# Deformable convolution, layer 2: convolution tiles split by tap parity, x planes and even taps on ScalarE

## The chip, the core and the metric

The kernel runs on one core of a Trainium2 chip. A core has TensorE for matrix products (PE in the rows: its weight loads stand apart as PEld), VectorE (DVE), ScalarE (ACT), GpSimd (POOL) and SyncE (SP), which here only starts transfers. The engines run their own instruction lists and meet at semaphores. The metric is the device time of one execution of the whole program in microseconds.

## What is computed

Four layers run on a batch of 4 images of 64 channels by 48 x 48 pixels. The change touches the second one only. In that layer two deformable 3x3 convolutions (index v below) read the same image, each with its own offsets:

```python
def deform_conv(x, offset, w, b):
    off = offset.reshape(B, K2, 2, H, W)
    dy, dx = (off[:, :, 0], off[:, :, 1])
    ...
    py = base_y.astype(x.dtype) + dy
    px = base_x.astype(x.dtype) + dx
    sampled = bilinear_gather(x, py, px)
    out = jnp.einsum('bckhw,ock->bohw', sampled, w.reshape(O, C, K2))
    return out + b[None, :, None, None]
```

Each of the 9 taps of each output pixel is a bilinear sample of the image; then a plain product over 64 channels and 9 taps follows, and a bias for each output channel.

## The kernel before

The touched function is `windows1`. It works in 24 chunks (`NQ`, 4 images times 6) of 8 rows by 48 pixels, 384 pixels (`CH`) each. A bilinear sample is written as a product with a small matrix of weights: each tile of 4 x 6 pixels takes its samples from a window of 10 x 12 pixels, so the contraction runs over 120 window places (`KW`), and a weight is the product of a hat function in y and one in x. For one chunk the stages are these.

- **Placement** (`place`, line 1455 on TensorE): two products of 384 columns for each half write the distances of the samples from the window places. ScalarE takes the magnitude (`magnitude`, L1539, 768 columns), VectorE turns it into hats in place (`hats_of`, L1578).
- **Nine steps** t = 0 to 8 (`STEPS`), each for two of the 18 samples (9 taps, two convolutions). `spread` (L1476) is four products of 32 rows by 120 columns of weights and 384 moving columns; they write two y planes to `p_y[t % 2]` and two x planes to `p_x`. Before the weights can be formed, the x planes are copied to `xs`: ScalarE copies plane 0 (`keep_x`, L1546), VectorE plane 1 (L1583). Then VectorE multiplies the y planes in PSUM by the x planes in SBUF (L1588, 768 columns) and writes the sampling weights `bmat`. There is one `p_x` (banks 4 and 5 of PSUM), so the next `spread` waits until both planes are out.
- **Eight sampling products** (`sample`, L1494), four matmuls of 216 columns each, use the weights of the chunk before; ScalarE moves their result to `smp` (`keep`, L1553). In the list of TensorE they alternate with the steps: `spread(n+1, t)`, `sample(n, t)`.
- **The convolution** (`conv`, L1510): for each tap four matmuls on the 64 x 64 quadrants of the array, convolution v on rows 64v, pixel half h on columns 64h, 192 moving columns each. They accumulate over the nine taps in PSUM banks 2 and 3 (`pc[v]`), which are also `p_y[1]`; three taps run before the second placement of chunk n+2, six behind it. VectorE adds the bias and writes the result in four pieces (`biased`, L1597).

An fp32 matmul stands in the records as two passes, with a weight load for each: a `spread` is 8 records, and the 36 matmuls of one `conv` are 72. All orders are written out by hand in the five engine lists; no scheduler moves anything. ScalarE's list in a chunk is `keep_x(n+1, t)`, `keep(n, t)` for t = 0 to 8, then the two magnitudes of chunk n+2. VectorE's is nine times copy and product, two hats, `biased(n)`. Chunk 0 has its nine steps alone in front, and chunk 23 its sampling alone at the end.

Of the kernel before, what the change touches and what calls it, by code (L numbers as in the profile page):

```python
# [6 lines left out]
ALU = mybir.AluOpType  # L7
# [15 lines left out]
TAPS = 9  # L23
# [1384 lines left out]
def windows1(nc, k, o3, bmat, win, sc, smp, hats, xs):  # L1408
# [7 lines left out]
         ("loaded0", "loaded1", "places", "absed", "hats", "spread", "x0_out", "x1_out", "weights", "sampled", "kept", "conv", "sc")}  # L1416
# [10 lines left out]
    pc = [ps[:, 512 * (2 + v):512 * (2 + v) + CH // 2] for v in range(2)]  # L1427
    S4 = smp.rearrange("p (s y x) -> p s y x", s=TAPS, y=ROWS)
    hat = hats.rearrange("p (q n) -> p q n", q=4)

    with nc.Block() as block:
# [14 lines left out]
        def _(pe):  # L1446
            def place(m, half):
                if half == 0:
                    if m >= 2:
                        pe.wait_ge(S["kept"], (m - 1) * PAIRS)  # L1450
                elif m:
                    pe.wait_ge(S["x0_out"], m * STEPS)
                    pe.wait_ge(S["x1_out"], m * STEPS)
# [5 lines left out]
            def spread(m, t):  # L1459
# [3 lines left out]
                else:  # L1463
                    pe.wait_ge(S["x0_out"], g)
                    pe.wait_ge(S["x1_out"], g)
# [14 lines left out]
            def sample(n, i):  # L1480
                if i == 0:
                    pe.wait_ge(S["weights"], (n + 1) * STEPS)
                    pe.wait_ge(S[f"loaded{n % 2}"], 64 * (n // 2 + 1))
                    if n + 1 < NQ:
                        pe.wait_ge(S["absed"], 2 * (n + 2))
# [13 lines left out]
            def conv(n, taps):  # L1499
# [5 lines left out]
                for t in taps:  # L1505
                    for v in range(2):
                        own = slice(64 * v, 64 * v + 64)
                        for h in range(2):
                            at = CH * t + CH // 2 * h
                            mm = pe.matmul(pc[v][64 * h:64 * h + 64, :], k["dws"][own, t, :], smp[own, at:at + CH // 2],  # L1510
                                           start=(t == 0), stop=(t == TAPS - 1), skip_group_check=True)
# [9 lines left out]
            for n in range(NQ):  # L1521
# [5 lines left out]
                if n + 2 < NQ:  # L1527
                    place(n + 2, 0)
                    conv(n, range(0, 3))
                    place(n + 2, 1)  # L1530
                    conv(n, range(3, TAPS))
# [4 lines left out]
        def _(act):  # L1536
# [4 lines left out]
            def keep_x(m, t):  # L1541
# [4 lines left out]
                act.activation(xs[t % 2][:, 0:CH], p_x[:, 0, :], ACT.Copy).then_inc(S["x0_out"], 1)  # L1546

            def keep(n, i):
                band, pair = divmod(i, NTX // 2)
                act.wait_ge(S["sampled"], n * PAIRS + i + 1)  # L1550
                if i == 0 and n:
# [3 lines left out]
                    .then_inc(S["kept"], 1)  # L1555

# [6 lines left out]
            for n in range(NQ):  # L1563
# [5 lines left out]
                if n + 2 < NQ:  # L1569
                    magnitude(n + 2, 0)  # L1570
                    magnitude(n + 2, 1)

        @block.vector
        def _(v_):
            def hats_of(m, half):
                v_.wait_ge(S["absed"], 2 * m + half + 1)
                own = hat[:, 2 * half:2 * half + 2, :]
                v_.tensor_scalar(own, own, 1.0, 1.0, ALU.min, ALU.subtract).then_inc(S["hats"], 1)  # L1578

            def weight(m, t):  # L1580
                g = m * STEPS + t
                v_.wait_ge(S["spread"], g + 1)
                v_.tensor_copy(xs[t % 2][:, CH:2 * CH], p_x[:, 1, :]).then_inc(S["x1_out"], 1)  # L1583
                v_.wait_ge(S["x1_out"], g + 1)
                v_.wait_ge(S["x0_out"], g + 1)
# [1030 lines left out]
```

## Time and profile before

| what | us |
|---|---|
| median of 3 runs | 1517.17 |
| lowest, highest | 1516.56, 1517.31 |
| the profiled execution | 1518.79 |
| its span in the trace | 1517.0 |
| TensorE, VectorE, ScalarE, GpSimd busy in the span | 1226.1, 1058.5, 637.0, 418.1 |
| `windows1` in the span, first placement to last bias | about 399 to 889.4 |

The page gives each engine's busy time, then the span in 40 slices, then groups of instructions. A row of the groups names line, engine, operation, what is written and read, partitions by elements, the count, busy time and mean duration, and behind the bar the idle time ahead of it with its releaser. A row of the timeline gives start, length, engine and count, and in brackets the idle time ahead. The 24 chunks repeat each other closely, so that one chunk can be read for all.

### The profile page before, as it was taken

To read this page: it belongs to the slowest core of one execution; us is meant where nothing else is said; L and a number is where in the kernel's file an instruction comes from. 1 tells how busy PE (TensorE), PEld (TensorE's weight loads), DVE (VectorE), ACT (ScalarE), POOL (GpSimd) and SP (SyncE) were. 2 spreads that over 40 slices of the span, in tenths; PEclk is the share of its full clock that TensorE was granted. 3 is DMA by queue.
4 is the path that set the end of the run, shared out by engine and by line. 5 is a ranking of instruction groups with operands and counts; after the bars stand their busy time and mean duration, and the time that the engine had idled before them with its cause. 6 is when DMAs were issued, how large, how long until landed. Compare 5 with 4: busy or idle time off the path is not lost. (4 is left out here: it accounts for less than half of the span.)

```text
span 1517.0 us, 32058 instructions
## 1 busy us (share of the span) xinstructions
PE 1226.1 (81%) x13604; PEld 605.8 (40%) x13604; DVE 1058.5 (70%) x1310; ACT 637.0 (42%) x1003; POOL 418.1 (28%) x272
## 2 busy tenths in 40 slices
PE   3860089959499999999999958879999999999558
PEld 1430077734134444444444434423333333334233
DVE  2679935568678888888888856864666767676623
ACT  1534035345345555555555524514444444445410
POOL 2001011222100000000000001118888888888400
PEclk9985599979589999999999978779999999999779
DMA  4100000002100000000000000400000000000132
GB/s 81 17 1 0 0 3 3 2 27 58 40 14 28 27 28 27 28 27 28 26 18 25 28 2 0 125 1 1 1 1 2 1 2 2 2 1 2 50 37 64
DMA packets 29071, 31.50 MB, mean 21 GB/s; under 512 B 19340, under 2 KB 21837, under 8 KB 28157
## 3 DMA queue, kind: packets, MB, share of 16 engines
q1 hardware_dynamic: 28925, 29.41, 7.8%
q8 instruction: 109, 1.79, 0.5%
q14 instruction: 37, 0.30, 0.1%
HBM read 21.07 MB, written 5.35 MB: 17 GB/s over the span
## 5 line engine op out<-in xcount | busy, mean ns | idle before, releaser
L2072 POOL TENSOR_TENSOR arena_sb<-arena_sb 128x768 f32<-128x768 f32 x168 | 323.0, 1923 | 121.6 <-ACT arena_sb L2033 101.1
L2087 DVE TENSOR_REDUCE arena_sb<-ps 128x4 f32<-128x1536 f32 x108 | 188.6, 1758 | 129.4 <-PE ps L1929 128.1
L2033 ACT ACTIVATE arena_sb<-ps 128x768 f32<-128x768 f32 x216 | 174.8, 810 | 243.1 <-PE ps L1962 241.0
L1476 PE MATMUL ps<-xp_sb,arena_sb 32*120 32x384 f32 x1728 | 207.0, 549 | 25.0 <-DVE arena_sb L1583 21.9
L1588 DVE TENSOR_TENSOR arena_sb<-ps,arena_sb 120x768 f32<-120x768 f32 x216 | 206.8, 957 | 8.2 <-DVE arena_sb L1583 0.8
L1962 PE MATMUL ps<-arena_sb 33*64 33x384 f32 x1728 | 187.5, 502 | 11.3 <-ACT arena_sb L2033 5.4
L1494 PE MATMUL ps<-arena_sb 120*64 120x216 f32 x1536 | 182.3, 359 | 0.0
L1974 PE MATMUL ps<-arena_sb 64*64 64x384 f32 x1728 | 168.0, 488 | 3.4 <-ACT arena_sb L2040 3.4
L1546 ACT ACTIVATE arena_sb<-ps 120x384 f32<-120x384 f32 x216 | 105.9, 490 | 148.7 <-PE ps L1476 148.7
L1583 DVE COPY arena_sb<-ps 120x384 f32<-120x384 f32 x216 | 120.4, 558 | 43.6 <-PE ps L1476 40.7
L1765 POOL MEMSET arena_sb<- 128x64 f32 x1 | 0.2, 151 | 544.8 <-POOLq L210 544.8
L1494 PEld LDWEIGHTS ps<-arena_sb 120*64 120x64 f32 x1536 | 93.2, 136 | 119.8 <-ACT xp_sb L1553 77.4
L1553 ACT ACTIVATE xp_sb<-ps 128x432 f32<-128x432 f32 x192 | 101.8, 530 | 74.7 <-PE ps L1494 74.7
L1929 PE MATMUL ps<-arena_sb 32*128 32x384 f32 x864 | 110.1, 584 | 15.6 <-DVE arena_sb L2087 9.6
L1476 PEld LDWEIGHTS ps<-xp_sb,arena_sb 32*120 32x120 f32 x1728 | 67.7, 182 | 101.3 <-ACT arena_sb L1546 65.7
L1962 PEld LDWEIGHTS ps<-arena_sb 33*64 33x64 f32 x1728 | 58.1, 134 | 110.1 <-ACT arena_sb L2033 86.0
L1974 PEld LDWEIGHTS ps<-arena_sb 64*64 64x64 f32 x1728 | 67.5, 134 | 78.8 <-issue 72.9
L610 PE MATMUL ps<-ident_sb,arena_sb 128*32 128x128 f32 x576 | 19.3, 289 | 77.9 <-PEq L472 77.9
L1510 PE MATMUL ps<-xp_sb,arena_sb 64*64 64x192 f32 x1728 | 80.8, 328 | 0.7 <-ACT xp_sb L1553 0.6
L1929 PEld LDWEIGHTS ps<-arena_sb 32*128 32x128 f32 x864 | 37.2, 199 | 87.3 <-issue 44.6
L1510 PEld LDWEIGHTS ps<-xp_sb,arena_sb 64*64 64x64 f32 x1728 | 61.8, 133 | 18.7 <-issue 14.0
L1597 DVE TENSOR_SCALAR arena_sb<-ps,dbs_sb 64x192 f32<-64x192 f32 x96 | 39.9, 416 | 27.4 <-PE ps L1510 26.4
(228 smaller groups left out, 1478.0 us busy)
## 6 DMA issues: line engine op xcount, KB each, us to landing
arena_sb<-pixel_major SPq DMA_DIRECT2D x96, 120.0 KB, 2.3
pixel_major<-arena_sb SPq DMA_DIRECT2D x24, 108.0 KB
x_sb<-in_x SPq DMA_DIRECT2D x4, 576.0 KB, 9.1
arena_sb<-arena_sb SPq DMA_DIRECT2D x8, 288.0 KB, 6.0
xn_sb<-in_W SPq DMA_DIRECT2D x1, 2304.0 KB, 8.1
arena_sb<-in_W SPq DMA_DIRECT2D x1, 2304.0 KB, 8.2
out_x<-x_sb SPq DMA_DIRECT2D x24, 96.0 KB, 2.2
arena_sb<-arena_sb SPq DMA_DIRECT2D x16, 36.0 KB, 3.7
```

Source lines behind the costliest of these rows:

```text
L1476: mm = pe.matmul(out, k["spr"][32 * row:32 * row + 32, q, :], hat[32 * row:32 * row + 32, slot, :], start=True, stop=True)
L1494: mm = pe.matmul(out[64 * v:64 * v + 64, :, :, IW * t:IW * t + IW], win[n % 2][0:KW, band, tile, :], weights[:, TAPS * v:TAPS * v + TAPS, ...
L1510: mm = pe.matmul(pc[v][64 * h:64 * h + 64, :], k["dws"][own, t, :], smp[own, at:at + CH // 2], start=(t == 0), stop=(t == TAPS - 1), skip_ ...
L1546: act.activation(xs[t % 2][:, 0:CH], p_x[:, 0, :], ACT.Copy).then_inc(S["x0_out"], 1)
L1583: v_.tensor_copy(xs[t % 2][:, CH:2 * CH], p_x[:, 1, :]).then_inc(S["x1_out"], 1)
L1588: v_.tensor_tensor(bmat[m % 2][:, 2 * CH * t:2 * CH * t + 2 * CH].rearrange("p (e n) -> p e n", e=2), p_y[t % 2], xs[t % 2].rearrange("p ( ...
L1929: mm = pe.matmul(p_m(m)[:, u, :], q4[own, CH * ib + PT * a:CH * ib + PT * a + PT], k4[own, CH * jc:CH * jc + CH], start=True, stop=True)
L1962: mm = pe.matmul(p_scores(g)[64 * i:64 * i + 64, h, :], kp[own, key:key + 64], qp[own, PIX * b2 + CH * ib:PIX * b2 + CH * ib + CH], start= ...
L1974: mm = pe.matmul(p_o[64 * h:64 * h + 64, i, :], at[64 * i:64 * i + 64, b2 * TPI + j, 64 * h:64 * h + 64], pt[g % SLOTS][64 * i:64 * i + 64 ...
L2033: act.activation(pt[g % SLOTS].rearrange("p (h n) -> p h n", h=2), p_scores(g), ACT.Exp)\
L2072: pool.tensor_tensor(acc, first, pt[g % SLOTS], ALU.add).then_inc(S["pool_added"], 1)
L2087: v.tensor_reduce(part.rearrange("p (a u j) -> p a u j", a=3, u=NB)[:, a, :, jc], p_m(m), AX.X, ALU.max)\
```

## The change

- `spread`, `sample` and the placements stay as they are. In `keep_x` ScalarE copies both x planes in one instruction of 768 columns for steps 0 to 7, counted in `x_out` (2 for the two planes). In step 8 the copy is split as before: ScalarE takes plane 0, VectorE plane 1 (`x_half`). VectorE's copies of steps 0 to 7 are gone.
- `conv` has two matmuls for each tap instead of four, one for each convolution, on all 384 columns. Even taps (0, 2, 4, 6, 8) go to the array's columns 0 to 63 and so to PSUM partitions 0 to 63, odd taps (1, 3, 5, 7) to columns and partitions 64 to 127. 18 matmuls in place of 36. Four taps run before the second placement instead of three.
- The two partial sums are now added: `even_taps` on ScalarE copies the even sum with the bias to `sc` (two instructions of 64 x 384), then `biased` on VectorE adds the odd sum (two of 64 x 384, one operand in PSUM and one in SBUF). `biased` waits for `even` in place of `conv`.
- `sample` waits for `hats` where it waited for `absed`; the `spread` just ahead of it waits for the same value already.

TensorE's list around one chunk's turn, before:

```order
456 L1476 MATMUL ps<-xp_sb,arena_sb 120x384 x4
457 L1494 MATMUL ps<-arena_sb 64x36x6 x4
458 L1476 MATMUL ps<-xp_sb,arena_sb 120x384 x4
459 L1455 MATMUL ps<-arena_sb 128x384 x2
460 L1510 MATMUL ps<-xp_sb,arena_sb 64x192 x12
461 L1455 MATMUL ps<-arena_sb 128x384 x2
462 L1510 MATMUL ps<-xp_sb,arena_sb 64x192 x24
463 L1476 MATMUL ps<-xp_sb,arena_sb 120x384 x4
```

The same place of TensorE's list now (L1483 is `spread`, L1501 `sample`, L1463 `place`, L1516 `conv`):

```order
456 L1483 MATMUL ps<-xp_sb,arena_sb 120x384 x4
457 L1501 MATMUL ps<-arena_sb 64x36x6 x4
458 L1483 MATMUL ps<-xp_sb,arena_sb 120x384 x4
459 L1463 MATMUL ps<-arena_sb 128x384 x2
460 L1516 MATMUL ps<-xp_sb,arena_sb 64x384 x8
461 L1463 MATMUL ps<-arena_sb 128x384 x2
462 L1516 MATMUL ps<-xp_sb,arena_sb 64x384 x10
463 L1483 MATMUL ps<-xp_sb,arena_sb 120x384 x4
```

Nothing changes places; the two pieces of the convolution hold 8 and 10 matmuls of 384 columns where they held 12 and 24 of 192.

ScalarE's list at the same turn, before:

```order
277 L1553 ACTIVATE xp_sb<-ps 128x9x4x12
278 L1546 ACTIVATE arena_sb<-ps 120x384
279 L1539 ACTIVATE xp_sb<-ps 128x768 x2
280 L1546 ACTIVATE arena_sb<-ps 120x384
281 L1553 ACTIVATE xp_sb<-ps 128x9x4x12
```

ScalarE's list now (L1553 is the copy of both planes, L1555 that of step 8, L1569 the even taps, L1562 `keep`, L1545 the magnitude):

```order
282 L1562 ACTIVATE xp_sb<-ps 128x9x4x12
283 L1555 ACTIVATE arena_sb<-ps 120x384
284 L1545 ACTIVATE xp_sb<-ps 128x768 x2
285 L1569 ACTIVATE arena_sb<-ps,dbs_sb 64x384 x2
286 L1553 ACTIVATE arena_sb<-ps 120x768
287 L1562 ACTIVATE xp_sb<-ps 128x9x4x12
```

Two instructions with the bias stand ahead of the first copy of the next chunk, and that copy has 768 columns.

VectorE's list at the turn, before, and after it the same place now (L1606 is the product, L1601 the copy of step 8, L1595 the hats, L1614 the adding):

```order
442 L1583 COPY arena_sb<-ps 120x384
443 L1588 TENSOR_TENSOR arena_sb<-ps,arena_sb 120x768
444 L1578 TENSOR_SCALAR xp_sb<-xp_sb 128x768 x2
445 L1597 TENSOR_SCALAR arena_sb<-ps,dbs_sb 64x192 x4
446 L1583 COPY arena_sb<-ps 120x384
447 L1588 TENSOR_TENSOR arena_sb<-ps,arena_sb 120x768
```

```order
381 L1606 TENSOR_TENSOR arena_sb<-ps,arena_sb 120x768 x8
382 L1601 COPY arena_sb<-ps 120x384
383 L1606 TENSOR_TENSOR arena_sb<-ps,arena_sb 120x768
384 L1595 TENSOR_SCALAR xp_sb<-xp_sb 128x768 x2
385 L1614 TENSOR_TENSOR arena_sb<-ps,arena_sb 64x384 x2
386 L1606 TENSOR_TENSOR arena_sb<-ps,arena_sb 120x768 x8
```

Eight products now follow each other without a copy between them, and four additions of a bias became two additions of planes.

The diff:

```diff
--- before.py
+++ after.py
@@ -1413,7 +1413,7 @@
 
     ps = k["psum"]
     S = {n: signal(k, "win_" + n) for n in
-         ("loaded0", "loaded1", "places", "absed", "hats", "spread", "x0_out", "x1_out", "weights", "sampled", "kept", "conv", "sc")}
+         ("loaded0", "loaded1", "places", "absed", "hats", "spread", "x_out", "x_half", "weights", "sampled", "kept", "conv", "even", "sc")}
     NQ = NB * CPI
     NTX = WW // IW
     PAIRS = 2 * (NTX // 2)
@@ -1424,9 +1424,13 @@
     p_x = ps[0:KW, 2048:3072].rearrange("p (e n) -> p e n", e=2)[:, :, 0:CH]
     p_place = [ps[:, at:at + 1024].rearrange("p (e n) -> p e n", e=2)[:, :, 0:CH] for at in (3072, 2048)]
     pq = [ps[:, 512 * (6 + i):512 * (6 + i) + TAPS * IH * 2 * IW] for i in range(2)]
-    pc = [ps[:, 512 * (2 + v):512 * (2 + v) + CH // 2] for v in range(2)]
+    pc = [ps[:, 512 * (2 + v):512 * (2 + v) + CH] for v in range(2)]
     S4 = smp.rearrange("p (s y x) -> p s y x", s=TAPS, y=ROWS)
     hat = hats.rearrange("p (q n) -> p q n", q=4)
+
+    def x_count(steps):
+
+        return 2 * steps - steps // STEPS
 
     with nc.Block() as block:
         @block.sync
@@ -1444,13 +1448,17 @@
 
         @block.tensor
         def _(pe):
+            def x_free(count):
+                pe.wait_ge(S["x_out"], x_count(count))
+                if count >= STEPS:
+                    pe.wait_ge(S["x_half"], count // STEPS)
+
             def place(m, half):
                 if half == 0:
                     if m >= 2:
                         pe.wait_ge(S["kept"], (m - 1) * PAIRS)
                 elif m:
-                    pe.wait_ge(S["x0_out"], m * STEPS)
-                    pe.wait_ge(S["x1_out"], m * STEPS)
+                    x_free(m * STEPS)
                 for e in range(2):
                     mm = pe.matmul(p_place[half][:, e, :], k["selp"][:, 2 * half + e, :], o3[:, CH * m:CH * m + CH],
                                    start=True, stop=True)
@@ -1461,8 +1469,7 @@
                 if t == 0:
                     pe.wait_ge(S["hats"], 2 * (m + 1))
                 else:
-                    pe.wait_ge(S["x0_out"], g)
-                    pe.wait_ge(S["x1_out"], g)
+                    x_free(g)
                 if t < 2 and m:
                     pe.wait_ge(S["weights"], m * STEPS)
                 elif t >= 2:
@@ -1482,7 +1489,7 @@
                     pe.wait_ge(S["weights"], (n + 1) * STEPS)
                     pe.wait_ge(S[f"loaded{n % 2}"], 64 * (n // 2 + 1))
                     if n + 1 < NQ:
-                        pe.wait_ge(S["absed"], 2 * (n + 2))
+                        pe.wait_ge(S["hats"], 2 * (n + 2))
                 if n * PAIRS + i >= 2:
                     pe.wait_ge(S["kept"], n * PAIRS + i - 1)
                 band, pair = divmod(i, NTX // 2)
@@ -1503,12 +1510,11 @@
                         pe.wait_ge(S["sc"], n)
                     pe.wait_ge(S["weights"], (n + 1) * STEPS + (STEPS - 1 if n + 1 < NQ else 0))
                 for t in taps:
+                    h = t % 2
                     for v in range(2):
                         own = slice(64 * v, 64 * v + 64)
-                        for h in range(2):
-                            at = CH * t + CH // 2 * h
-                            mm = pe.matmul(pc[v][64 * h:64 * h + 64, :], k["dws"][own, t, :], smp[own, at:at + CH // 2],
-                                           start=(t == 0), stop=(t == TAPS - 1), skip_group_check=True)
+                        mm = pe.matmul(pc[v][64 * h:64 * h + 64, :], k["dws"][own, t, :], smp[own, CH * t:CH * t + CH],
+                                       start=(t < 2), stop=(t >= TAPS - 2), skip_group_check=True)
                 if taps[-1] == TAPS - 1:
                     mm.then_inc(S["conv"], 1)
 
@@ -1526,9 +1532,9 @@
                         sample(n, t)
                 if n + 2 < NQ:
                     place(n + 2, 0)
-                    conv(n, range(0, 3))
+                    conv(n, range(0, 4))
                     place(n + 2, 1)
-                    conv(n, range(3, TAPS))
+                    conv(n, range(4, TAPS))
                 else:
                     conv(n, range(TAPS))
 
@@ -1543,7 +1549,10 @@
                 act.wait_ge(S["spread"], g + 1)
                 if g >= 2:
                     act.wait_ge(S["weights"], g - 1)
-                act.activation(xs[t % 2][:, 0:CH], p_x[:, 0, :], ACT.Copy).then_inc(S["x0_out"], 1)
+                if t < STEPS - 1:
+                    act.activation(xs[t % 2].rearrange("p (e n) -> p e n", e=2), p_x, ACT.Copy).then_inc(S["x_out"], 2)
+                else:
+                    act.activation(xs[t % 2][:, 0:CH], p_x[:, 0, :], ACT.Copy).then_inc(S["x_out"], 1)
 
             def keep(n, i):
                 band, pair = divmod(i, NTX // 2)
@@ -1553,6 +1562,13 @@
                 act.activation(S4[:, :, IH * band:IH * band + IH, 2 * IW * pair:2 * IW * pair + 2 * IW],
                                pq[i % 2].rearrange("p (s y x) -> p s y x", s=TAPS, y=IH), ACT.Copy)\
                     .then_inc(S["kept"], 1)
+
+            def even_taps(n):
+                act.wait_ge(S["conv"], n + 1)
+                for v in range(2):
+                    last = act.activation(sc.rearrange("p h n -> p (h n)")[64 * v:64 * v + 64, CH * n:CH * n + CH],
+                                          pc[v][0:64, :], ACT.Identity, bias=k["dbs"][0:64, v + 1:v + 2])
+                last.then_inc(S["even"], 1)
 
             magnitude(0, 0)
             magnitude(0, 1)
@@ -1569,20 +1585,22 @@
                 if n + 2 < NQ:
                     magnitude(n + 2, 0)
                     magnitude(n + 2, 1)
+                even_taps(n)
 
         @block.vector
         def _(v_):
             def hats_of(m, half):
+                own = hat[:, 2 * half:2 * half + 2, :]
                 v_.wait_ge(S["absed"], 2 * m + half + 1)
-                own = hat[:, 2 * half:2 * half + 2, :]
                 v_.tensor_scalar(own, own, 1.0, 1.0, ALU.min, ALU.subtract).then_inc(S["hats"], 1)
 
             def weight(m, t):
                 g = m * STEPS + t
-                v_.wait_ge(S["spread"], g + 1)
-                v_.tensor_copy(xs[t % 2][:, CH:2 * CH], p_x[:, 1, :]).then_inc(S["x1_out"], 1)
-                v_.wait_ge(S["x1_out"], g + 1)
-                v_.wait_ge(S["x0_out"], g + 1)
+                if t == STEPS - 1:
+                    v_.wait_ge(S["spread"], g + 1)
+                    v_.tensor_copy(xs[t % 2][:, CH:2 * CH], p_x[:, 1, :]).then_inc(S["x_half"], 1)
+                    v_.wait_ge(S["x_half"], m + 1)
+                v_.wait_ge(S["x_out"], x_count(g + 1))
                 if t == 0 and m >= 2:
                     v_.wait_ge(S["sampled"], (m - 1) * PAIRS)
                 v_.tensor_tensor(bmat[m % 2][:, 2 * CH * t:2 * CH * t + 2 * CH].rearrange("p (e n) -> p e n", e=2),
@@ -1590,13 +1608,10 @@
                     .then_inc(S["weights"], 1)
 
             def biased(n):
-                v_.wait_ge(S["conv"], n + 1)
+                v_.wait_ge(S["even"], n + 1)
                 for v in range(2):
-                    for h in range(2):
-                        at = CH * n + CH // 2 * h
-                        last = v_.tensor_scalar(sc.rearrange("p h n -> p (h n)")[64 * v:64 * v + 64, at:at + CH // 2],
-                                                pc[v][64 * h:64 * h + 64, :], k["dbs"][64 * h:64 * h + 64, v + 1:v + 2], None,
-                                                ALU.add)
+                    own = k["sc"].rearrange("p h n -> p (h n)")[64 * v:64 * v + 64, CH * n:CH * n + CH]
+                    last = v_.tensor_tensor(own, pc[v][64:128, :], own, ALU.add)
                 last.then_inc(S["sc"], 1)
 
             hats_of(0, 0)
@@ -1609,9 +1624,9 @@
                 if n + 1 < NQ:
                     for t in range(STEPS):
                         weight(n + 1, t)
-                if n + 2 < NQ:
-                    hats_of(n + 2, 0)
-                    hats_of(n + 2, 1)
+                    if n + 2 < NQ:
+                        hats_of(n + 2, 0)
+                        hats_of(n + 2, 1)
                 biased(n)
```

## Rows read from the trace of the kernel before

**Rows 1.** Page, the span in 40 slices: busy tenths, and TensorE's granted clock

```profile
PE   3860089959499999999999958879999999999558
PEclk9985599979589999999999978779999999999779
```

**Rows 2.** Stretches: us, busy and count per engine, clock, DMA share, GB/s

```profile
core 0: us, PE busy (x) PEld busy (x) DVE busy (x) ACT busy (x) POOL busy (x), PEclk, DMA share, GB/s
240.00:300.00 60.00, 54.67 (x1202) 45.31 (x1190) 33.70 (x61) 29.10 (x48) 8.23 (x16) 1.00 0.01 2
485.00:868.00 383.00, 368.33 (x4136) 182.75 (x4128) 318.64 (x470) 198.05 (x370) 0.00 (x0) 1.00 0.09 26
```

**Rows 3.** Timeline of one inner step, from 552.6 (start, length, engine, line)

```profile
552.61 0.92 PE L1476 MATMUL ps<-xp_sb,arena_sb 32*120 32x384 f32 x8
553.46 0.95 PE L1494 MATMUL ps<-arena_sb 120*64 120x216 f32 x8
553.60 0.49 ACT L1546 ACTIVATE arena_sb<-ps 120x384 f32<-120x384 f32 x1 [0.34 <-PE ps L1476]
553.60 0.56 DVE L1583 COPY arena_sb<-ps 120x384 f32<-120x384 f32 x1 [0.18 <-PE ps L1476]
554.34 0.30 PEld L1476 LDWEIGHTS ps<-xp_sb,arena_sb 32*120 32x120 f32 x8 [0.32 <-ACT arena_sb L1546]
```

**Rows 4.** Timeline of a chunk's turn, 541 to 549

```profile
541.21 1.21 PE L1510 MATMUL ps<-xp_sb,arena_sb 64*64 64x192 f32 x24
...
542.77 2.18 PE L1510 MATMUL ps<-xp_sb,arena_sb 64*64 64x192 f32 x48
542.88 0.81 ACT L1539 ACTIVATE xp_sb<-ps 128x768 f32<-128x768 f32 x1 [0.76 <-PE ps L1455]
543.72 0.56 DVE L1578 TENSOR_SCALAR xp_sb<-xp_sb 128x768 f32<-128x768 f32 x1 [0.79 <-ACT xp_sb L1539]
544.88 0.30 PEld L1476 LDWEIGHTS ps<-xp_sb,arena_sb 32*120 32x120 f32 x8 [0.28 <-issue]
...
545.02 1.71 DVE L1597 TENSOR_SCALAR arena_sb<-ps,dbs_sb 64x192 f32<-64x192 f32 x4 [0.74 <-PE ps L1510]
...
546.76 0.56 DVE L1583 COPY arena_sb<-ps 120x384 f32<-120x384 f32 x1
...
547.39 0.33 PEld L1476 LDWEIGHTS ps<-xp_sb,arena_sb 32*120 32x120 f32 x8 [1.09 <-issue]
...
548.39 0.49 ACT L1546 ACTIVATE arena_sb<-ps 120x384 f32<-120x384 f32 x1 [1.13 <-PE ps L1476]
```

**Rows 5.** Timeline of two steps of chunk 0, no sampling between them

```profile
404.30 0.52 PEld L1476 LDWEIGHTS ps<-xp_sb,arena_sb 32*120 32x120 f32 x8 [1.90 <-ACT arena_sb L1546]
...
406.03 0.56 DVE L1583 COPY arena_sb<-ps 120x384 f32<-120x384 f32 x1 [0.85 <-PE ps L1476]
...
406.66 0.52 PEld L1476 LDWEIGHTS ps<-xp_sb,arena_sb 32*120 32x120 f32 x8 [1.85 <-ACT arena_sb L1546]
```

**Rows 6.** Groups of the whole span: busy and mean ns, then idle before

```profile
L1539 ACT ACTIVATE xp_sb<-ps 128x768 f32<-128x768 f32 x48 | 38.8, 810 | 23.5 <-PE ps L1455 23.5
```

**Rows 7.** Timeline: two activations with a bias, 384 columns

```profile
336.52 1.05 ACT L1230 ACTIVATE arena_sb<-ps,offb_sb 128x384 f32<-128x384 f32 x2 [11.10 <-PE ps L1185]
```

**Rows 8.** One line, the fourth layer's addition from PSUM: min/median/max ns

```profile
L2280 DVE TENSOR_TENSOR x_sb<-x_sb,ps x24: 545/552/558, 1483.0 to 1513.8; 64x384 f32<-64x384 f32 x24
```

**Rows 9.** Timeline of the third layer: quadrants of 64 x 64 with 384 columns

```profile
1201.36 1.47 PE L1974 MATMUL ps<-arena_sb 64*64 64x384 f32 x16
...
1205.10 1.15 PE L1974 MATMUL ps<-arena_sb 64*64 64x384 f32 x12
```

**Rows 10.** Timeline of the last two chunks' ends

```profile
874.36 3.15 PE L1510 MATMUL ps<-xp_sb,arena_sb 64*64 64x192 f32 x72
...
887.72 1.71 DVE L1597 TENSOR_SCALAR arena_sb<-ps,dbs_sb 64x192 f32<-64x192 f32 x4 [8.44 <-PE ps L1510]
```

## The prediction, made before the changed kernel had run

> **What bounds the kernel now.** I read the slices of the page first. From slice 12 to 23 TensorE is 9 tenths busy or more and its clock is granted in full [rows 1]. The table of stretches says it for the inner chunks alone: 368.33 of 383 us for TensorE (96%), 318.64 for VectorE (83%), 198.05 for ScalarE (52%), clock 1.00 [rows 2]. Shares do not say what a longer instruction on ScalarE costs, so the timeline of one step comes next. The period is 552.61 to 554.34, 1.73 us. `spread` runs until 553.53, `sample` starts at 553.46 and runs until 554.41, and the next `spread` loads its weights at 554.34 [rows 3]. TensorE has no hole. But both copies start at 553.60, 0.99 after the `spread` began, and VectorE's ends at 554.16. Since one `p_x` serves all steps, the next `spread` could start at the earliest 0.07 later, at 554.23. The slack is only 0.11 us. The 0.07 is how long TensorE takes to go on after a copy: 546.76 + 0.56 = 547.32 to 547.39 [rows 4], and 406.03 + 0.56 = 406.59 to 406.66 [rows 5].
>
> A chunk lasts 19.61 us: 2.51 from its first `spread` to the second (544.88 to 547.39 [rows 4]), seven steps of 1.73, and the rest with step 8, placements and convolution. The 2.51 has a hole on TensorE, since VectorE first does its four biases, 1.71 us, and only then the copy [rows 4].
>
> **1. Both planes on ScalarE.** VectorE loses 0.56 us a step, but it was not the last to end a step; TensorE's own work was. ScalarE's copy grows from 0.49 [rows 3] to 768 columns, which take 0.81 from PSUM to SBUF in the same stage [rows 6]. The two planes went out beside each other in 0.56; now they go out one behind the other in 0.81. The path is: weight load to copy 0.99 (with idle time ahead of it 1.00: 547.39 to 548.39 [rows 4]), copy 0.81, on to TensorE 0.07. That is 1.88 instead of 1.73, so +0.15. ScalarE isn't itself full: 0.81 + 0.53 of 1.88; its `keep` follows the end of `sample`, some 1.85 after the `spread`'s start, when the copy has just ended. VectorE's product of 0.96 runs beside it. Seven such intervals a chunk (steps 1 to 8; the first is item 4) in 22 chunks, and six in the chunk in which the clock rises, are 160 x 0.15 = +24.0. Bounds: if TensorE goes on 0.03 after ScalarE, as VectorE does (542.88 + 0.81 = 543.69 to 543.72 [rows 4]), the step is 1.84 and the term +17.6; with 0.10 for the handing over it is +28.8. I take 0.07 since it was read for this very wait.
>
> The Trainium skill, page "TensorEngine Tiling (Array Packing)", section "PSUM Bottleneck", speaks against this part: after tiling, emptying PSUM can become the limit, and both ScalarE and VectorE should be used for it. The rows above agree, 0.56 side by side against 0.81 on one engine.
>
> **2. The same in chunk 0.** There no sampling lies between the steps, and the wait decides already: load to copy 1.73 (404.30 to 406.03), copy 0.56, on 0.07, together 2.36, at half clock [rows 5]. With 0.81 it is 2.61: 8 x 0.25 = +2.0. Nothing hides it.
>
> **3. The convolution.** The records say whether it is held by columns or by instructions. 24 records (three taps) span 1.21 us and 48 span 2.18 [rows 4], 72 span 3.15 [rows 10]: 0.97 for 24, so four quadrants together need 0.162 for a pass of 192 columns, and a tap 0.323. The third layer has just the new shape, 64 x 64 with 384 columns: 16 records in 1.47, 12 in 1.15, so 0.32 for four together [rows 9]. Twice the columns take twice the time; fewer matmuls save nothing. Two taps now fill the four quadrants for 2 x 0.32 = 0.65 us, and nine taps make five rounds, the last with two quadrants idle: 5 x 0.65 = 3.25 against 9 x 0.323 = 2.91, some +0.33 a chunk. In 24 chunks +7.8. It lies on TensorE, the engine without a hole, so all of it counts. Bounds: 0 (should tap 8 find room somewhere) and +12, a round at 0.68.
>
> The Trainium skill has a rule for the other side: the same page, section "Instruction Overhead", gives each matmul about 60 cycles of overhead. As an estimate from that page, 18 matmuls fewer would give back 18 x 25 ns = 0.45 us a chunk, 10.8 in all, and turn this term into about -3. The rows don't show such a cost.
>
> **4. The start of a chunk.** From the first `spread` on: the conv's end reaches the next engine at +0.14 (545.02 [rows 4]); two activations with a bias take 1.05 [rows 7]; on to VectorE 0.03 [rows 4]; two additions of 0.552 from PSUM [rows 8]; on to TensorE 0.07. The second `spread` waits for `sc`, because `p_y[1]` lies on the convolution's banks, so it starts at 0.14 + 1.05 + 0.03 + 1.10 + 0.07 = 2.39. ScalarE's first copy is ready before, at 0.14 + 1.05 + 0.81 = 2.00. Against 2.51 this is -0.12; I take -0.10, 22 times: -2.2. With the two activations at 0.49 each without extra cost the chain is 2.32 (-4.2 in all), with 0.65 each 2.64 (+2.9). VectorE does the first product after the additions, until about 3.3; it is wanted before the third `spread` at 4.3.
>
> **5. Nothing or little.** The fourth tap ahead of the second placement moves that placement, the second magnitude and the second hats by 0.33; the hats end at 544.28 and are wanted at 544.88 [rows 4], and this moves by 0.33 too. `hats` for `absed`: the `spread` in front waits for it anyway. At the end of the last chunk 1.71 [rows 10] becomes 1.05 + 0.03 + 1.10, +0.5; in the chunk before, the even taps hold ScalarE when the first `keep` is due, +0.2. The transfers (DMA share 0.09 [rows 2]) wait for `sampled` alone. No table load is added on ScalarE: the list of instructions has none.
>
> **Sum.** 24.0 + 2.0 + 7.8 - 2.2 + 0.7 = +32.3. The profiled execution took 1518.8 with a span of 1517.0, 1.6 above the median. 1518.8 + 32.3 = 1551.1; against the median, 1517.2 + 32.3 = **1549.5**.
>
> **The rivals.**
> - The step isn't lengthened: TensorE prepares the next `spread` under the copy so that 0.81 fits. For it: 0.15 is little. Against: chunk 0 shows load, copy and wait in series without overlap. Then items 1 and 2 vanish: 1549.5 - 26 = 1523.5.
> - Faster than before: the convolution is held by its matmuls rather than its columns, and halving them halves it. It gives 24 x 1.46 = -35.1 in place of +7.8: 1506.6. For it: each record carries its own weight load. Against: rows 9. It decides from the point where a convolution saves (24.0 + 2.0 - 2.2 + 0.7)/24 = 1.02 us; around that point lies "no change".
> - The parity split doesn't do what it says: the tiles of one tap pair with each other but not with those of the next, since these come later in the list. Then nine taps cost 9 x 0.65 = 5.85, +2.94 x 24 = 70.6 in place of 7.8: 1612. Against: passes of successive `values` matmuls overlap four by four in rows 9.
> - The holes cost clock. A step gets a hole of 0.15 in 1.88, 8%. A stretch with TensorE 91% busy kept clock 1.00 [rows 2], which speaks against it. If 3 of the 24 chunks ran at 1.2 GHz, each up to 19 us longer since TensorE is busy nearly throughout, the time would be up to 1549.5 + 57 = 1606.5.
>
> **How the numbers follow.** Forecast 0.80, step hidden 0.06, convolution halved 0.05, saving near the break-even point 0.03, parity without overlap 0.03, clock 0.03. The bounds of the terms put together (steps -6.4 to +4.8, convolution -7.8 to +4, start of a chunk -2 to +5, and about 3 for where the clock changes fall in other stages) give, not all at one end, 1538 to 1560. This holds the forecast's case nearly whole, and what lies outside is under 2 in 10. A measurement of this kernel tells about 0.2% (3 us) from no change. Faster by more 0.05, within 0.03, slower 0.92.
>
> **What would show it.** Steps: `spread` every 1.88 instead of 1.73, TensorE's idle time ahead of it released by ScalarE's copy, some 0.15 each. Chunk 0: 2.61. Convolution: 20 records in the larger piece, 0.32 for every four, whole 3.25. First interval of a chunk 2.4. VectorE's busy time in the stage down by more than 100 us while the time rises. The prediction is wrong if the step stays at 1.73 or the convolution gets shorter than 2.9.

## The result and the profile after

The changed kernel takes 1556.96 us in the median (1555.26 to 1559.24, 4 runs) against 1517.24 of the kernel before (1516.56 to 1518.8, 4 runs). The ratio is 1.0261 with a 95% interval of 1.0243 to 1.0279: slower by 2.6%, 39.7 us. The span of the profiled execution went from 1517.0 to 1555.6, +38.6.

From the page of the changed kernel, TensorE's and VectorE's slices, then the groups of line, operation, shapes and count, busy and mean ns, and idle time ahead with its releaser:

```profile
PE   3850199868499999999999977689999999999558
DVE  3769845659445555555555546684666666677723
...
L1606 DVE TENSOR_TENSOR arena_sb<-ps,arena_sb 120x768 f32<-120x768 f32 x216 | 206.8, 957 | 174.9 <-ACT arena_sb L1553 172.2
...
L1553 ACT ACTIVATE arena_sb<-ps 120x768 f32<-120x768 f32 x192 | 155.5, 810 | 120.1 <-PE ps L1483 95.1
...
L1483 PEld LDWEIGHTS ps<-xp_sb,arena_sb 32*120 32x120 f32 x1728 | 67.4, 182 | 139.1 <-ACT arena_sb L1553 121.5
```

The same slices of VectorE in the kernel before:

```profile
DVE  2679935568678888888888856864666767676623
```

The stage is recognisable by VectorE, which falls from 8 tenths to 4 and 5. Its products wait 172.2 us for ScalarE's copies. That by itself costs nothing, since VectorE isn't the engine that holds the step; what counts is the last row, where the weight loads of the next `spread` wait for the same copies. The 192 copies of two planes take 0.810 each, as the magnitudes do in [rows 6]. The stretch that [rows 2] shows of before, now:

```profile
485.00:868.00 383.00, 356.22 (x3192) 147.15 (x3192) 205.20 (x254) 249.82 (x381) 0.00 (x0) 1.00 0.08 24
```

In 383 us VectorE works 205.20 instead of 318.64, ScalarE 249.82 instead of 198.05, and TensorE 356.22 instead of 368.33 at the same full clock. TensorE, which had no hole inside a step, has holes there now. One step, to be laid beside [rows 3]:

```profile
561.78 0.92 PE L1483 MATMUL ps<-xp_sb,arena_sb 32*120 32x384 f32 x8
562.63 0.95 PE L1501 MATMUL ps<-arena_sb 120*64 120x216 f32 x8
562.82 0.81 ACT L1553 ACTIVATE arena_sb<-ps 120x768 f32<-120x768 f32 x1 [0.56 <-PE ps L1483]
563.63 0.53 ACT L1562 ACTIVATE xp_sb<-ps 128x432 f32<-128x432 f32 x1
563.66 0.96 DVE L1606 TENSOR_TENSOR arena_sb<-ps,arena_sb 120x768 f32<-120x768 f32 x1 [0.94 <-ACT arena_sb L1553]
563.68 0.30 PEld L1483 LDWEIGHTS ps<-xp_sb,arena_sb 32*120 32x120 f32 x8 [0.49 <-ACT arena_sb L1553]
```

The period is 561.78 to 563.68, 1.90 us (before 1.73). ScalarE's copy ends at 563.63, and 0.05 later TensorE loads the next weights; `sample` had ended at 563.58, and ahead of the weight load the loader's idle time has grown from 0.32 to 0.49. The chunk's turn, to be laid beside [rows 4]:

```profile
551.43 1.52 PE L1516 MATMUL ps<-xp_sb,arena_sb 64*64 64x384 f32 x16
...
553.32 2.15 PE L1516 MATMUL ps<-xp_sb,arena_sb 64*64 64x384 f32 x20
...
555.40 0.30 PEld L1483 LDWEIGHTS ps<-xp_sb,arena_sb 32*120 32x120 f32 x8 [0.60 <-DVE xp_sb L1595]
...
555.52 1.16 ACT L1569 ACTIVATE arena_sb<-ps,dbs_sb 64x384 f32<-64x384 f32 x2 [1.28 <-PE ps L1516]
...
556.71 1.13 DVE L1614 TENSOR_TENSOR arena_sb<-ps,arena_sb 64x384 f32<-64x384 f32 x2 [1.89 <-ACT arena_sb L1569]
...
557.96 0.33 PEld L1483 LDWEIGHTS ps<-xp_sb,arena_sb 32*120 32x120 f32 x8 [1.15 <-ACT arena_sb L1553]
```

The convolution's first piece, with four taps instead of three, spans 1.52 where it spanned 1.21; the second, with five instead of six, 2.15 where it spanned 2.18. From the first `spread` to the second it is 555.40 to 557.96, 2.56 (before 2.51). A whole chunk went from 19.62 to 21.13.

### The profile page after: what moved, and what is told of

Same layout as the page of the kernel before. It is cut to its first block and busy times, and to the rows that moved or that the text cites. A ratio compares the mean times of both kernels' runs of the same rounds, so it can differ in the third digit from the quotient of the medians.

```text
span 1555.6 us, 29969 instructions
## 1 busy us (share of the span) xinstructions
PE 1249.5 (80%) x12740; PEld 576.6 (37%) x12740; DVE 938.8 (60%) x1070; ACT 723.6 (47%) x1051; POOL 418.1 (27%) x272
## 5 line engine op out<-in xcount | busy, mean ns | idle before, releaser
L1606 DVE TENSOR_TENSOR arena_sb<-ps,arena_sb 120x768 f32<-120x768 f32 x216 | 206.8, 957 | 174.9 <-ACT arena_sb L1553 172.2
L1483 PE MATMUL ps<-xp_sb,arena_sb 32*120 32x384 f32 x1728 | 206.9, 549 | 44.2 <-DVE arena_sb L1614 17.4
L1553 ACT ACTIVATE arena_sb<-ps 120x768 f32<-120x768 f32 x192 | 155.5, 810 | 120.1 <-PE ps L1483 95.1
L1501 PE MATMUL ps<-arena_sb 120*64 120x216 f32 x1536 | 182.3, 359 | 0.2 <-ACT xp_sb L1562 0.2
L1501 PEld LDWEIGHTS ps<-arena_sb 120*64 120x64 f32 x1536 | 93.2, 136 | 120.2 <-ACT xp_sb L1562 77.6
L1944 PE MATMUL ps<-arena_sb 32*128 32x384 f32 x864 | 115.4, 610 | 11.3 <-DVE arena_sb L2102 5.3
L1483 PEld LDWEIGHTS ps<-xp_sb,arena_sb 32*120 32x120 f32 x1728 | 67.4, 182 | 139.1 <-ACT arena_sb L1553 121.5
L1562 ACT ACTIVATE xp_sb<-ps 128x432 f32<-128x432 f32 x192 | 101.7, 530 | 3.1 <-PE ps L1501 2.6
L1516 PE MATMUL ps<-xp_sb,arena_sb 64*64 64x384 f32 x864 | 87.7, 493 | 0.8 <-ACT xp_sb L1562 0.6
L1614 DVE TENSOR_TENSOR arena_sb<-ps,arena_sb 64x384 f32<-64x384 f32 x48 | 26.9, 560 | 54.3 <-ACT arena_sb L1569 53.9
L1545 ACT ACTIVATE xp_sb<-ps 128x768 f32<-128x768 f32 x48 | 38.9, 812 | 30.3 <-PE ps L1463 30.3
L1185 PE MATMUL ps<-xp_sb,offw_sb 64*64 64x384 f32 x432 | 39.9, 516 | 9.4 <-PEq L210 9.4
```

Source lines behind the costliest of these rows:

```text
L1483: mm = pe.matmul(out, k["spr"][32 * row:32 * row + 32, q, :], hat[32 * row:32 * row + 32, slot, :], start=True, stop=True)
L1501: mm = pe.matmul(out[64 * v:64 * v + 64, :, :, IW * t:IW * t + IW], win[n % 2][0:KW, band, tile, :], weights[:, TAPS * v:TAPS * v + TAPS, ...
L1553: act.activation(xs[t % 2].rearrange("p (e n) -> p e n", e=2), p_x, ACT.Copy).then_inc(S["x_out"], 2)
L1562: act.activation(S4[:, :, IH * band:IH * band + IH, 2 * IW * pair:2 * IW * pair + 2 * IW], pq[i % 2].rearrange("p (s y x) -> p s y x", s=T ...
L1606: v_.tensor_tensor(bmat[m % 2][:, 2 * CH * t:2 * CH * t + 2 * CH].rearrange("p (e n) -> p e n", e=2), p_y[t % 2], xs[t % 2].rearrange("p ( ...
L1944: mm = pe.matmul(p_m(m)[:, u, :], q4[own, CH * ib + PT * a:CH * ib + PT * a + PT], k4[own, CH * jc:CH * jc + CH], start=True, stop=True)
```

## The experiments

Each is compared with the kernel before on its own chip. The starts of the x copies in each trace give the step and the whole chunk, in us, alike in nearly all chunks:

| kernel | ratio to before | inner step | chunk |
|---|---|---|---|
| before | 1 | 1.73 | 19.62 |
| the changed kernel | 1.0261 | 1.90 | 21.13 |
| changed, copies count by one | 1.0184 | 1.85 | 20.79 |
| changed, tap 8 in halves | 1.0200 | 1.90 | 20.85 |
| convolution alone | 1.0141 | 1.73 | 20.51 |
| copies alone | 1.0120 | 1.90 | 20.25 |
| before, copies count by two | 1.0007 | 1.73 | 19.62 |
| before, biases split | 0.9882 | 1.73 | 18.81 |
| biases split, placements together | 0.9887 | 1.73 | 18.81 |

**The wait that doesn't fit.** In the changed kernel the copy of two planes starts 1.04 us after its `spread` (561.78 to 562.82), where both old copies and the copy of step 8 start after 0.99. In the records of the changed kernel a wait instruction for the `spread` stands by itself ahead of this copy; the other copies carry that wait themselves. The difference in the source is the increment by 2. On ScalarE a wait instruction (for `weights`) stands ahead of the copy in every kernel, so there is no instruction more: with the increment by 2 it holds the wait for the `spread` too, and the copy itself waits for nothing.

```diff
-        return 2 * steps - steps // STEPS
+        return steps
...
-  act.activation(xs[t % 2]..., p_x, ACT.Copy).then_inc(S["x_out"], 2)
+  act.activation(xs[t % 2]..., p_x, ACT.Copy).then_inc(S["x_out"], 1)
```

> The changed kernel, except that the copy of both x planes raises x_out by 1 instead of 2, and the waits count steps. Theory: the increment by 2 costs the instruction its own wait; a separate wait instruction stands ahead of it, and the copy starts 1.04 us after the spread instead of 0.99. Then the step falls from 1.90 to 1.85, and 168 steps x 0.05 = 8.4 give 1548.6. Rival: the 0.05 belongs to the reading of two planes (768 columns in two banks); then nothing moves, 1557.

Measured: 1548.37 against 1520.05 of the kernel before on that chip, ratio 1.0184 (1.0167 to 1.0201). One step of this kernel:

```profile
558.75 0.92 PE L1483 MATMUL ps<-xp_sb,arena_sb 32*120 32x384 f32 x8
559.74 0.81 ACT L1553 ACTIVATE arena_sb<-ps 120x768 f32<-120x768 f32 x1 [0.45 <-PE ps L1483]
560.60 0.30 PEld L1483 LDWEIGHTS ps<-xp_sb,arena_sb 32*120 32x120 f32 x8 [0.44 <-ACT arena_sb L1553]
```

0.99, 0.81 and 0.05: the step is 1.85. The stretch from the first x copy to the last fell from 507.30 to 498.83, 8.5 us less; the theory had 8.4. Of the 8.5, 0.3 is a single long step that only the changed kernel's trace has (see the last section); 8.2 come from one number in the source, 0.05 in each of the 168 steps. The 0.05 belongs to the separate wait, and reading two banks costs nothing extra. By the two ratios it is 0.8% of 1517, 11.7 us; the intervals of the ratios leave room for 8.5.

**The same number where there is slack.** The kernel before, with both split copies counting by two.

```diff
-  act.activation(xs[t % 2][:, 0:CH], p_x[:, 0, :], ACT.Copy).then_inc(S["x0_out"], 1)
+  act.activation(xs[t % 2][:, 0:CH], p_x[:, 0, :], ACT.Copy).then_inc(S["x0_out"], 2)
-  v_.tensor_copy(xs[t % 2][:, CH:2 * CH], p_x[:, 1, :]).then_inc(S["x1_out"], 1)
+  v_.tensor_copy(xs[t % 2][:, CH:2 * CH], p_x[:, 1, :]).then_inc(S["x1_out"], 2)
```

> The kernel before, with both split copies raising their semaphores by 2 and all their waits doubled; the work is the same. Theory: each copy now starts 1.04 us after its spread instead of 0.99 on ScalarE, and later on VectorE too if it behaves alike. In a step VectorE's copy then ends at 1.60 and TensorE could go on at 1.67, still under the 1.73 of its own work: steps stay 1.73. Only where the wait decides does the time grow: chunk 0 by 8 x 0.05, and at the first step of a chunk nothing where the wait is long fulfilled. 1517.6, no change that can be measured. Rival: there is no slack in the step and 168 x 0.05 = 8.4 come on top, 1525.6.

Measured: ratio 1.0007 (0.9996 to 1.0018), no change. The step in its timeline:

```profile
552.12 0.92 PE L1476 MATMUL ps<-xp_sb,arena_sb 32*120 32x384 f32 x8
552.97 0.95 PE L1494 MATMUL ps<-arena_sb 120*64 120x216 f32 x8
553.16 0.49 ACT L1546 ACTIVATE arena_sb<-ps 120x384 f32<-120x384 f32 x1 [0.39 <-PE ps L1476]
553.18 0.56 DVE L1583 COPY arena_sb<-ps 120x384 f32<-120x384 f32 x1 [0.18 <-PE ps L1476]
553.77 0.96 DVE L1588 TENSOR_TENSOR arena_sb<-ps,arena_sb 120x768 f32<-120x768 f32 x1
553.85 0.30 PEld L1476 LDWEIGHTS ps<-xp_sb,arena_sb 32*120 32x120 f32 x8 [0.32 <-ACT arena_sb L1546]
```

The copies start at 1.04 and 1.06 now, VectorE's ends at 553.74, and the step is still 1.73. The two delays are real and cost an ordinary step nothing, because 0.11 of slack was there. In chunk 0, where the wait decides, the step rose from 2.37 to 2.43. The stretch from the first x copy to the last still grew from 470.8 to 473.0, too little to show in the ratio: 0.6 in chunk 0, 0.5 in chunk 1, and the rest in five single steps that took 1.81 to 2.06.

**The convolution alone.** The kernel before with the new convolution, even taps and additions; the x planes are copied one by each engine as before.

```diff
-  for h in range(2):
-      at = CH * t + CH // 2 * h
-      mm = pe.matmul(pc[v][64 * h:64 * h + 64, :], k["dws"][own, t, :], smp[own, at:at + CH // 2], start=(t == 0), ...)
+  h = t % 2
+  mm = pe.matmul(pc[v][64 * h:64 * h + 64, :], k["dws"][own, t, :], smp[own, CH * t:CH * t + CH], start=(t < 2), ...)
```

> The kernel before with the new convolution, even taps on ScalarE and odd taps added by VectorE, and the x planes copied one by each engine as before. Theory (columns set the convolution): +0.29 us a chunk on TensorE, 7.0 in all; and VectorE's first copy of a chunk now stands behind even taps and additions, 0.14 + 1.16 + 0.03 + 1.13 + 0.56 + 0.07 = 3.09 us in place of 2.51, 22 x 0.58 = 12.8; with 0.7 at the end 1517.2 + 20.5 = 1537.7. Rival (matmuls set the convolution, 60 cycles each): 10.8 less, 1527. Rival (the convolution is halved): 1496.

Measured: 1541.14, ratio 1.0141 (1.0124 to 1.0158); on the 1517.24 of before that is 1538.6, as the column theory has it. Its turn of a chunk:

```profile
546.97 0.30 PEld L1476 LDWEIGHTS ps<-xp_sb,arena_sb 32*120 32x120 f32 x8 [0.60 <-DVE xp_sb L1585]
...
547.09 1.16 ACT L1559 ACTIVATE arena_sb<-ps,dbs_sb 64x384 f32<-64x384 f32 x2 [1.28 <-PE ps L1509]
...
548.28 1.13 DVE L1603 TENSOR_TENSOR arena_sb<-ps,arena_sb 64x384 f32<-64x384 f32 x2 [1.89 <-ACT arena_sb L1559]
...
549.45 0.56 DVE L1590 COPY arena_sb<-ps 120x384 f32<-120x384 f32 x1
...
550.08 0.33 PEld L1476 LDWEIGHTS ps<-xp_sb,arena_sb 32*120 32x120 f32 x8 [1.70 <-issue]
```

The diff shows the convolution alone; `even_taps` and the additions are those of the changed kernel. Even taps, additions and copy stand one behind the other, and the second `spread` comes 3.11 after the first. Both rivals with cheaper matmuls fall: 1527 would have been a ratio of 1.0065, and 1496 one below 1.

**Where the convolution's loss sits.** The changed kernel, with tap 8 computed in two halves of 192 columns, one on each column half of the array.

```diff
+  if t < TAPS - 1:
...
+      continue
+  for h in range(2):
+      at = CH // 2 * h
+      mm = pe.matmul(pc[v][64 * h:64 * h + 64, at:at + CH // 2], k["dws"][own, t, :], smp[own, CH * t + at:CH * t + at + CH // 2], start=False, stop=True, ...)
```

> The changed kernel, with tap 8 alone computed in two halves of 192 columns on both column halves of the array (four matmuls), so that no quadrant is idle in the last round; the sum over both planes stays the same. Theory (two idle quadrants in the fifth round are the whole loss of the convolution): its larger piece is 0.32 us shorter, 24 x 0.32 = 7.7 less than the changed kernel: 1549.3, ratio 1.0210. Rival (the loss comes from 384-column passes): nothing moves, ratio 1.0261. Rival (a cost for each matmul): two matmuls more make it a little slower.

Measured: ratio 1.02 (1.0187 to 1.0214); expected was 1.0210. The second piece of its convolution:

```profile
552.50 1.52 PE L1517 MATMUL ps<-xp_sb,arena_sb 64*64 64x384 f32 x16
553.84 0.51 PE L1522 MATMUL ps<-xp_sb,arena_sb 64*64 64x192 f32 x8
554.28 0.60 PE L1483 MATMUL ps<-xp_sb,arena_sb 32*120 32x384 f32 x4
```

From the piece's start to the next `spread` it is 1.78 instead of 2.08 (553.32 to 555.40), and a chunk has 20.85 instead of 21.13. From step 8 to the next chunk's first `spread` it is 4.94, where the kernel before has 4.96 and the changed kernel 5.25. So the loss is the fifth round with two quadrants idle, not the longer passes. With two matmuls more in each convolution (20 instead of 18) it got faster.

**The copies alone.** The changed kernel with the old convolution and the old biases.

```diff
-  h = t % 2
-  mm = pe.matmul(pc[v][64 * h:64 * h + 64, :], k["dws"][own, t, :], smp[own, CH * t:CH * t + CH], start=(t < 2), ...)
+  for h in range(2):
+      at = CH * t + CH // 2 * h
+      mm = pe.matmul(pc[v][64 * h:64 * h + 64, :], k["dws"][own, t, :], smp[own, at:at + CH // 2], start=(t == 0), ...)
...
-  even_taps(n)
...
-  last = v_.tensor_tensor(own, pc[v][64:128, :], own, ALU.add)
+  last = v_.tensor_scalar(sc..., pc[v][64 * h:64 * h + 64, :], k["dbs"][64 * h:64 * h + 64, v + 1:v + 2], None, ALU.add)
```

> The changed kernel with the old convolution and the old four biases on VectorE: of the change only the copies of both x planes on ScalarE are left. Theory: steps 1.90 instead of 1.73, 160 x 0.17 = 27, chunk 0 +2.1; the first interval of a chunk shrinks, as no copy of VectorE's stands behind the biases any more: spread to copy 1.04, copy 0.81, on 0.07 = 1.92 instead of 2.51, 22 x -0.59 = -13.0. 1517.2 + 16.1 = 1533.3. Rival (the copies carry the whole loss): 1517.2 + 32 = 1549 or more.

Measured: 1537.82, ratio 1.012 (1.0103 to 1.0137), 1535.4 on the 1517.24; the 1533.3 expected would be 1.0106. Its turn of a chunk:

```profile
551.49 0.92 PE L1483 MATMUL ps<-xp_sb,arena_sb 32*120 32x384 f32 x8
551.63 1.71 DVE L1608 TENSOR_SCALAR arena_sb<-ps,dbs_sb 64x192 f32<-64x192 f32 x4 [0.74 <-PE ps L1517]
...
552.52 0.81 ACT L1554 ACTIVATE arena_sb<-ps 120x768 f32<-120x768 f32 x1 [2.23 <-PE ps L1483]
...
553.48 0.92 PE L1483 MATMUL ps<-xp_sb,arena_sb 32*120 32x384 f32 x8 [0.19 <-DVE arena_sb L1608]
```

The gain at the turn is there: from weight load to weight load (551.49 to 553.45, just ahead of the last row) it is 1.97 in place of 2.51, since VectorE has no copy to make behind its biases. It is 0.05 more than the 1.92 expected: the second `spread` waits for the biases, which end at 553.34, and starts 0.11 later. Seven steps of 1.90 give more than that away. The two halves of the change add up: 1.0141 and 1.0120 above 1 make 1.0261, which is the whole change. At the turn one half loses 0.60 and the other gains 0.54; the whole change loses 0.05 there.

**What VectorE's load was worth.** The kernel before, with the biases of one convolution moved to ScalarE and nothing else.

```diff
+  def bias_of(n):
+      act.wait_ge(S["conv"], n + 1)
+      for h in range(2):
+          at = CH * n + CH // 2 * h
+          last = act.activation(sc...[0:64, at:at + CH // 2], pc[0][64 * h:64 * h + 64, :], ACT.Identity, bias=k["dbs"][64 * h:64 * h + 64, 1:2])
+      last.then_inc(S["sc_act"], 1)
...
-  for v in range(2):
-      for h in range(2):
+  for h in range(2):
...
-      last = v_.tensor_scalar(sc...[64 * v:64 * v + 64, at:at + CH // 2], pc[v][64 * h:64 * h + 64, :], ...)
+      last = v_.tensor_scalar(sc...[64:128, at:at + CH // 2], pc[1][64 * h:64 * h + 64, :], ...)
```

TensorE waits for `sc_act` wherever it waits for `sc`.

> The kernel before, with the biases of the first convolution moved to ScalarE (two instructions of 64 x 192 behind the magnitudes) and those of the second left on VectorE (two). Theory: the only hole of TensorE in a chunk is VectorE's 1.71 us of biases ahead of its first copy; halved, the copy starts at 1.0 and the first interval falls from 2.51 to TensorE's own 1.75. 22 x -0.76 = -16.7, end -0.6: 1500. Rival: another wait (ScalarE's copy behind its biases, 0.14 + 1.0 + 0.49 + 0.07 = 1.70, if an activation with a bias is dearer) keeps it at 2.0: 1506.

Measured: 1501.93, ratio 0.9882 (0.9864 to 0.99), 1499.3 on the 1517.24. The turn:

```profile
540.96 0.30 PEld L1477 LDWEIGHTS ps<-xp_sb,arena_sb 32*120 32x120 f32 x8 [0.28 <-issue]
...
541.10 0.84 ACT L1563 ACTIVATE arena_sb<-ps,dbs_sb 64x192 f32<-64x192 f32 x2 [1.33 <-PE ps L1512]
541.10 0.85 DVE L1607 TENSOR_SCALAR arena_sb<-ps,dbs_sb 64x192 f32<-64x192 f32 x2 [0.74 <-PE ps L1512]
...
541.98 0.56 DVE L1594 COPY arena_sb<-ps 120x384 f32<-120x384 f32 x1
...
542.69 0.30 PEld L1477 LDWEIGHTS ps<-xp_sb,arena_sb 32*120 32x120 f32 x8 [0.32 <-ACT arena_sb L1548]
```

The stretch of [rows 2] in this kernel:

```profile
485.00:868.00 383.00, 382.34 (x4328) 191.60 (x4324) 309.20 (x440) 223.55 (x428) 0.00 (x0) 1.00 0.09 26
```

The biases run side by side, the first interval is 1.73 like every other step, and TensorE works 382.34 of 383 us. This version is faster than both kernels, although it takes only 0.86 us a chunk from VectorE: that load stood in TensorE's one hole. The 0.56 a step that the changed kernel takes from VectorE stood in no hole; that it was worth nothing by itself is read from the step's timeline, no run takes it away without loading ScalarE instead.

**One change of tile kind less.** The kernel of the run before, with the first placement moved behind the first three taps.

```diff
-  place(n + 2, 0)
   conv(n, range(0, 3))
+  place(n + 2, 0)
   place(n + 2, 1)
```

> The kernel before with the biases split between ScalarE and VectorE as in the run before, and the first placement moved behind the first three taps, next to the second placement: TensorE changes between kinds of tiles three times in a chunk's turn instead of four. Theory: TensorE has no hole left, so each change of kind (0.1 us between the convolution's last pass and the placement) counts: 22 x 0.1 = 2.2 less than with the split biases alone, ratio 0.987. Rival: the first magnitude and hats come 1.1 us later and the next spread waits for the second hats, 0.1 to 0.3 a chunk: ratio 0.990 to 0.993.

Measured: ratio 0.9887 (0.9871 to 0.9902), the same as with the split biases alone. The saving was spent at once:

```profile
551.82 0.96 DVE L1599 TENSOR_TENSOR arena_sb<-ps,arena_sb 120x768 f32<-120x768 f32 x1
551.97 0.30 PEld L1477 LDWEIGHTS ps<-xp_sb,arena_sb 32*120 32x120 f32 x8 [0.32 <-ACT arena_sb L1548]
...
552.89 0.89 PEld L1512 LDWEIGHTS ps<-xp_sb,arena_sb 64*64 64x64 f32 x24 [0.62 <-ACT xp_sb L1555]
...
556.92 0.30 PEld L1477 LDWEIGHTS ps<-xp_sb,arena_sb 32*120 32x120 f32 x8 [0.28 <-DVE xp_sb L1589]
```

From step 8 to the next first `spread` it is 4.95, as without the move (4.96). The saving itself is there: the two placements side by side take 0.75 (554.06 to 554.81), where apart they took 0.43 and 0.44. But the convolution, which overwrites `p_y[1]`, now comes straight behind step 8 and starts 0.11 after VectorE's product of step 7 has ended (552.78). In the other order the placement stood in that time. That this wait is the releaser is read from the times and from the semaphore in the source; the row names ScalarE's `keep`, which had ended at 552.62. The changed kernel's trace supports the reading, where in the last chunk but one the convolution follows step 8 directly and the product of step 7 ends later:

```profile
909.61 0.96 DVE L1606 TENSOR_TENSOR arena_sb<-ps,arena_sb 120x768 f32<-120x768 f32 x1 [0.94 <-ACT arena_sb L1553]
909.63 0.92 PE L1483 MATMUL ps<-xp_sb,arena_sb 32*120 32x384 f32 x8
...
910.69 2.48 PEld L1516 LDWEIGHTS ps<-xp_sb,arena_sb 64*64 64x64 f32 x34 [0.76 <-ACT xp_sb L1562]
```

The convolution starts 1.06 after step 8 there instead of 0.92, and again 0.12 after the product's end (910.57). It keeps its distance to the product and not to step 8.

## Why the prediction was right, and where it was off

Forecast were 1549.5 us and +32.3; measured 1557.0 and +39.7, inside the range of 1538 to 1560 and on the forecast side. The mechanism of each term held, but the sum was 7 us short: the copies (1) and the start of a chunk (4) were each some 3 us too low, and only the convolution (3) was a little too high.

1. **Both planes on ScalarE: +24.0 forecast.** The step was forecast at 1.88 and is 1.90, and the first one after the turn 1.92. Six times 0.17 and once 0.16 are 1.18 a chunk in 22 chunks, and six times 0.17 in the one in which the clock rises: some +27. The path was right, but two of its parts were mis-sized in opposite directions: the start 1.04 instead of 0.99 (the wait taken out of the copy, shown by counting by one) and the handing over 0.05 instead of 0.07. The 0.07 was not read for this wait, as the prediction says: in both rows the copy that ends last is VectorE's, not ScalarE's. Its sum is also 0.01 off: 0.99, 0.81 and 0.07 make 1.87, and 1.88 takes the start at 1.00; the bounds of 1.84 and 28.8 do the same. The upper bound held the measured value.
2. **Chunk 0: +2.0 forecast.** From its first x copy to the next chunk's it went from 23.69 to 25.75, +2.1.
3. **Convolution: +7.8 forecast.** From step 8 to the next chunk's first `spread` it is 550.15 to 555.40, 5.25 instead of 4.96: +0.29 a chunk, 7.0. A convolution in one piece spans 3.44 (from 910.72 in the trace now) instead of 3.15, the same 0.29; why not the full 0.33 wasn't traced. The halved tap 8 shows that this is the fifth round. The estimate from the Trainium skill, page "TensorEngine Tiling (Array Packing)", section "Instruction Overhead", would have made this term about -3; in the run with the convolution alone no such saving is seen, and with two matmuls more, tap 8 in halves, the kernel got faster.
4. **The start of a chunk: -2.2 forecast.** This step failed in its sign. 2.39 was forecast and 2.56 came, +0.05 against before, 22 times +1.1. Three parts were too short: two activations with a bias 1.16 instead of 1.05 (each takes 0.574 and the second starts 0.59 after the first; the pair of [rows 7] took 0.58 each, but the second started 0.48 after the first, so they overlapped), additions 1.13 instead of 1.10, and from VectorE's end (557.84) to TensorE 0.12 instead of 0.07. The lead ahead of the activations was 0.12 instead of 0.14; together 0.12 + 1.16 + 0.03 + 1.13 + 0.12 = 2.56. The 0.12 behind VectorE stood in the copies alone too: 553.34 to 553.45, the weight load just ahead of 553.48. The 0.07 had been read for another wait.
5. **The end: +0.7 forecast.** The last even taps and additions take 2.32 from 924.93 to 927.25 where the biases took 1.71, +0.6, and before the last chunk's convolution `keep` is late by 0.3: +0.9.

The measured parts make 27 + 2.1 + 7.0 + 1.1 + 0.9 = 38.1 of the 38.6 by which the span grew. The stage itself, from the first x copy to the last addition, grew by the same 38.1, from 485.8 to 523.9; 0.3 of it is the long step of chunk 19, within the rounding of the parts. The other 0.5 lies outside the stage and wasn't traced further. Of the rivals none came: the step wasn't hidden, the convolution wasn't halved, successive taps do share the array, and the clock stayed at 1.00 with some 0.10 of idle time in each 1.90 (563.58 to 563.68).

## What to carry to other kernels

A busy share tells which engine to relieve only where that engine's end is waited for. Write down the path through one step, with each handing over, and see whose end is last. Here VectorE was 83% busy and its x copies were covered; putting two copies that ran side by side on one engine gave a covered 0.56 for an uncovered 0.81. What counts of it is only what goes over TensorE's own work, 0.17 a step. Half of the biases ahead of the first copy of a chunk was worth 18 us; the copies taken from VectorE in the other steps bought nothing that a run shows. And when work is tiled over parts of the array, count rounds, not instructions: nine equal pieces over two column halves leave half the array idle for one round.

## What the runs showed of the hardware

- A compute instruction that raises its semaphore by 2 had its own wait put into a separate instruction, and it started 0.05 us later (1.04 against 0.99 on ScalarE; 1.06 on VectorE). Counting by one took 8.2 us from the stage where the copy was on the critical path, and where there was slack the ratio didn't show it (1.0007). The Trainium skill, page "Trainium Kernel Development and Optimization", section "Key Constraints", says that compute semaphores must increment by 1; here an increment by 2 computed and ran, but was paid for.
- An activation of 64 x 384 with a bias from memory took 0.574 us where one of 120 x 384 without it took 0.490, and two of them started 0.59 apart, without overlap; in the pair of 128 x 384 of [rows 7] the second started 0.10 before the first had ended. What decides the overlap stays open.
- Now and then a copy started 0.28 to 0.35 us late behind a `spread` that had run in its usual time; in the changed kernel once, in chunk 19, where the step took 2.18 in place of 1.90. This goes with the count by two as well. The four traces whose copies count by two have seven such starts behind the first two chunks (one each in the changed kernel, with tap 8 in halves and in the copies alone, four in the kernel before counting by two, on ScalarE and on VectorE); the five traces that count by one have none. With one trace for each kernel, and no run made for it, the cause stays open.
